# A four-layer Perceiver kernel: earlier weight loads, biases off one-row products, one normalisation for two

## The reference, cut to what matters

```python
x = x + taylor(ln(x))            # L0_attn: causal, features 1, q, q*q; 4 weight matrices, no bias
# L0_ffn, first expert
logits = xt @ router_w + router_b; probs = softmax(logits)
gate, idx = max(probs), argmax(probs)
y = gate * (xt @ expert_w[idx] + expert_b[idx])
# L2_attn, one head over 256 channels
Q, K, V = x @ W1 + b1, x @ W2 + b2, x @ W3 + b3
out = softmax(Q K^T / 16) V @ W4 + b4
# L2_ffn: 8 zone experts, weights w from a router and a temperature
out = sum_e w_e * ((silu(x @ Wg_e) * (x @ Wu_e)) @ Wd_e)
# L3_attn, on ln(x): its own norm again, then two gates and a scan over tokens
normed = (x - mu) * rsqrt(var + EPS) * gamma + beta
z = sigmoid(normed @ Wg.T + bg); c = normed @ Wc.T + bc
h_t = (1 - z_t) * h_{t-1} + z_t * c_t;  out = hs + x
# L3_ffn
out = gelu(x @ w1 + b1) @ w2 + b2
```

## Time and profile before

| | |
|---|---|
| timed runs, median (lowest to highest), us | 1720.31 (1718.38 to 1727.86), 3 runs |
| profiled execution, its own time, us | 1728.6 |
| its span, us, and mean granted clock | 1726.8, 0.931 |
| busy: TensorE, VectorE, ScalarE, GpSimd | 89%, 57%, 42%, 22% |
| granted clock, 40 slices of 43.2 us, in tenths | 9999998799999996579999999889999688999998 |
| DMA busy, the same slices, in tenths | 7668785243453045035554076336660741466401 |

### The profile page before, as it was taken

How to read it: one execution, slowest core, us unless ns; L and a number is a source line. 1 busy time by engine, 2 the same in 40 slices (tenths; PEclk the granted TensorE clock), 3 DMA queues, 4 the chain that set the end, 5 groups by cost and what they waited for, 6 DMA issues and landing times. The chain is left out here.

```text
span 1726.8 us, 30618 instructions
## 1 busy us (share of the span) xinstructions
PE 1538.9 (89%) x11362; PEld 867.1 (50%) x11362; DVE 990.7 (57%) x2293; ACT 716.7 (42%) x961; POOL 381.9 (22%) x543
## 2 busy tenths in 40 slices
PE   6989886899999988979999988589999796999987
PEld 2644644355555555425555555235555464455544
DVE  2434433788888743267777424288884134888831
ACT  3233140244444422025565623147676111676741
POOL 7132140366666620010000012111010000110100
PEclk9999998799999996579999999889999688999998
DMA  7668785243453045035554076336660741466401
GB/s 239 207 218 253 224 258 151 55 70 57 63 73 61 1 82 114 1 65 80 78 78 79 2 240 183 96 71 99 96 98 2 134 147 40 67 100 96 72 19 55
DMA packets 130077, 178.00 MB, mean 103 GB/s; under 512 B 13947, under 2 KB 104972, under 8 KB 122767
## 3 DMA queue, kind: packets, MB, share of 16 engines
q1 hardware_dynamic: 126612, 173.55, 46.1%
q10 hardware_dynamic: 3328, 2.63, 0.6%
HBM read 132.31 MB, written 43.78 MB: 102 GB/s over the span
## 5 line engine op out<-in xcount | busy, mean ns | idle before, releaser
L708 ACT ACTIVATE prob_a<-ps 128x1024 f32<-128x1024 f32 x512 | 505.5, 1023 | 303.2 <-PE ps L593 216.3
L576 PE MATMUL ps<-kop,qop 116*128 116x512 bf16 x1024 | 341.5, 403 | 59.6 <-PEq L431 43.3
L721 DVE CUSTOM_DVE_ANT_0 dump_a<-ps,neg_q 128x512 bf16<-128x512 f32 (+1 forms) x485 | 328.6, 717 | 99.3 <-PE ps L576 97.8
L590 PE MATMUL ps<-qop,kop 116*128 116x256 bf16 x2048 | 349.1, 274 | 5.5 <-ACT prob_a L708 4.9
L725 DVE TENSOR_REDUCE best_a<-ps 128x1 f32<-128x512 f32 (+1 forms) x488 | 312.4, 707 | 58.4 <-PE ps L576 58.3
L590 PEld LDWEIGHTS ps<-qop,kop 116*128 116x128 bf16 x2048 | 194.9, 100 | 137.1 <-ACT prob_a L708 18.3
L576 PEld LDWEIGHTS ps<-kop,qop 116*128 116x128 bf16 x1024 | 86.7, 99 | 220.1 <-issue 99.9
L593 PE MATMUL ps<-neg_k,identb 128*128 128x512 bf16 x512 | 195.7, 382 | 0.0
L615 PE MATMUL ps<-prob_a,vop_a 128*32 128x256 f32 x3072 | 185.0, 382 | 0.0
L820 POOL TENSOR_TENSOR used_a<-prob_a,gT 128x1024 f32<-128x1024 f32 x64 | 151.6, 2369 | 88.1 <-DVE used_a L738 68.0
L311 PE MATMUL ps<-ctxT,wk 128*128 128x512 f32 x256 | 123.2, 628 | 36.8 <-DVE rest L362 23.7
(11 more groups left out here) (296 smaller groups left out, 1422.9 us busy)
## 6 DMA issues: line engine op xcount, KB each, us to landing
kop<-kparts SPq DMA_DIRECT2D x448, 128.0 KB, 5.2
kparts<-kp SPq DMA_DIRECT2D x64, 384.0 KB, 3.7
vals<-vst SPq DMA_DIRECT2D x16, 1024.0 KB, 6.8
vraw<-vals SPq DMA_DIRECT2D x64, 256.0 KB, 6.4
e_w<-in_e_w SPq DMA_DIRECT2D x6, 2048.0 KB, 16.4
z_w<-in_z_w SPq DMA_DIRECT2D x24, 256.0 KB, 5.9
ctxT<-in_ctxT SPq DMA_DIRECT2D x8, 512.0 KB, 9.2
raw<-in_mask SPq DMA_DIRECT2D x8, 512.0 KB, 5.8
```

The costliest lines, as they stand in the source:

```text
L576: return pe.matmul(out, qop[0:R_ALL, h, t * P:(t + 1) * P], kop[0:R_ALL, h % UNROLL, j * CHUNK:(j + 1) * CHUNK], start=True, stop=True)
L590: ins = pe.matmul(st_bank(n)[:, j * NT:(j + 1) * NT], kop[0:R_ALL, h % UNROLL, k * P:(k + 1) * P], qop[0:R_ALL, h, :], start=(j % 2 == 0), ...
L708: act.activation(prob[:, n % NP, :], st_bank(n), ACT.Exp).then_inc(S("exp_done"), 1)
L721: dve.tensor_tensor_reduce(out=dump[:, k % 2, 0:width], in0=bank, in1=c.neg_q[:, t, j * CHUNK:j * CHUNK + width], scale=1.0, scalar=-3.0e3 ...
```

## The change

**Weights.** Five classes (`TaylorWeights`, `FirstExpertWeights`, `PlainWeights`, `ZoneWeights`, `LastWeights` for the last two stages) hold SBUF tiles and semaphores that were inside the stages. They are made before the attention ahead of the stages, and their loads are issued on SP's queue in that attention, behind the operands of the last head. Their semaphores are cleared after the last stage that uses them.

**Biases.** first_expert: the router's bias is added by VectorE as it reads the logits; the experts' biases come from one product of the turned share (8 rows) with the 8 bias rows, after expert 5, added to `x` by VectorE ahead of expert 6. plain_attention: q's bias goes into ScalarE's read (scaled by GpSimd first), k's and v's into VectorE's read, the output's is added to `x` by GpSimd. recurrence: gate biases go into ScalarE's Sigmoid and VectorE's product. feed_forward: the output's bias is added to `x` by GpSimd. q, k and the gates are read in halves of 128 channels, each with its own count.

**Norm.** recurrence takes statistics once. From the variance v of `x` it forms v + EPS and v(1 + EPS) + EPS^2; GpSimd raises both to -1/2 in one instruction; one scale gives the single norm, the other the double. gamma and beta move to ScalarE's copy of the turned tile, one read for each 128 channels.

**Fillers and tables.** 12 filler products are issued during plain_attention's softmax and 12 during recurrence's scan; recurrence's opening fill is 16 products instead of 32. A one-element Exp, Sigmoid or Gelu opens ScalarE's list in plain_attention, recurrence and feed_forward.

The diff, cut to its core:

```diff
+SOFTMAX_FILL, SCAN_FILL = 12, 12
@@ attend, SP
                 ops.load(sp, l, h + UNROLL)
+            if load_next is not None:
+                load_next(sp)
             sp.wait_ge(S("weights"), 32 if l + 1 < LAYERS else 16)
@@ one of the five classes; the others are like it
+class FirstExpertWeights:
+    def load(self, sp):
+        a = self.c.a
+        sp.dma_start(self.router[:, :, :], tiles(a["f_router"])).then_inc(self.S("router"), 16)
+        sp.dma_start(self.router_b[:, :], a["f_router_b"].to_broadcast((P, E))).then_inc(self.S("router_b"), 16)
+        sp.dma_start(self.bias[:, :], a["f_bias"]).then_inc(self.S("bias"), 16)
+        for e in range(E):
+            sp.dma_start(self.w[:, e, :, :], tiles(a["f_w"][e, :, :])).then_inc(self.S(f"expert{e}"), 16)
@@ taylor, TensorE
-            pe.wait_ge(S("weights"), 64)
+            for name in ("q", "k", "v", "o"):
+                pe.wait_ge(weights.S(name), 16)
@@ first_expert, TensorE
             for e in range(E):
-                pe.wait_ge(S(f"expert{e}"), 16)
+                pe.wait_ge(weights.S(f"expert{e}"), 16)
                 if e >= 4:
                     pe.wait_ge(S("added"), QT * (e - 3))
-                by_tokens_pe(c, pe, halves(c, 2 + e % 4), c.xT, w[:, e, :, :], bias[0:1, e, :]).then_inc(S("e_psum"), 1)
+                by_tokens_pe(c, pe, halves(c, 2 + e % 4), c.xT, w[:, e, :, :], None).then_inc(S("e_psum"), 1)
+                if e == TURN_SHARE:     # 3
+                    pe.wait_ge(S("share_found"), QT)
+                    for t in range(QT):
+                        ins = pe.transpose(c.ps[0:E, 6, t * P:(t + 1) * P], share[:, t, :], c.ident[:, :])
+                    ins.then_inc(S("share_turned"), 1)
+                if e == ADD_BIAS:       # 5
+                    pe.wait_ge(S("shareT_ready"), 1)
+                    pe.wait_ge(weights.S("bias"), 16)
+                    for t in range(QT):
+                        ins = pe.matmul(halves(c, 7)[t], shareT[:, t * P:(t + 1) * P], weights.bias[:, :],
+                                        start=True, stop=True)
+                    ins.then_inc(S("bias_psum"), 1)
@@ plain_attention, TensorE
             for k, name in ((0, "q_psum"), (1, "k_psum")):
                 for m in range(CT):
-                    ins = by_channels_pe(c, pe, c.ps[:, 1 + k, m * NT:(m + 1) * NT],
-                                         lambda ct: w[:, k, ct, m * P:(m + 1) * P], c.xT, b[0:1, k, m * P:(m + 1) * P])
-                ins.then_inc(S(name), 1)
+                    by_channels_pe(c, pe, c.ps[:, 1 + 2 * k + m, 0:NT],
+                                   lambda ct: w[:, k, ct, m * P:(m + 1) * P], c.xT).then_inc(S(name), 1)
@@ plain_attention, TensorE, behind the scores
+            keep_warm(c, pe, SOFTMAX_FILL)
             pe.wait_ge(S("p_scaled"), QT)
@@ recurrence, GpSimd, TensorE, VectorE
-            norm_pool(c, pool, S)
-            norm_pool(c, pool, S, 1)
+            pool.wait_ge(S("norm_var"), 2)
+            pool.tensor_tensor(rstd[:, :, :], var[:, :, :], c.minus_half[:, :].unsqueeze(1).to_broadcast((P, 2, QT)), ALU.pow)\
+                .then_inc(S("norm_rstd"), 1)
...
-            keep_warm(c, pe, 2 * NORM_FILL)
-            pe.wait_ge(S("scaled"), 2 * QT)
+            keep_warm(c, pe, NORM_FILL)
+            pe.wait_ge(S("norm_done"), QT)
...
+            keep_warm(c, pe, SCAN_FILL)
             pe.wait_ge(S("scanned"), CT)
...
+            for t in range(QT):
+                dve.tensor_scalar(c.att[:, t, :], c.x[:, t, :], c.moments[:, t, 0:1], rstd[:, 1, t:t + 1],
+                                  ALU.subtract, ALU.mult).then_inc(S("norm_done"), 1)
@@ feed_forward, TensorE
-            by_tokens_pe(c, pe, halves(c, 7), hT, w2, b2[:, :], HT).then_inc(S("out_psum"), 1)
+            by_tokens_pe(c, pe, halves(c, 7), hT, w2, None, HT).then_inc(S("out_psum"), 1)
@@ program
+                    cross(c, 0, True, True, load_next)      # TaylorWeights, FirstExpertWeights
+            cross(c, 2, False, False, load_next)            # PlainWeights, ZoneWeights
+            cross(c, 3, False, False, weights.load)         # LastWeights
```

More of the change, by code:

```diff
@@ L1048, in _, with __init__, load, first_expert @@
             add_stream_dve(c, dve, S, 1)
-def first_expert(c):
+class FirstExpertWeights:
+    def __init__(self, c, ctx):
+        self.c = c
+        self.S = Sems(c.nc, ctx, "first_w")
+        sb = lambda name, shape: ctx.enter_context(c.nc.sbuf_tensor(f"f_{name}", shape, F32))
+        self.router = sb("router", [P, CT, E])
+        self.router_b = sb("router_b", [P, E])
+        self.bias = sb("bias", [E, D])
+        self.w = sb("w", [P, E, CT, D])
+    def load(self, sp):
+        a = self.c.a
[4 more added lines that the diff above has]
+            sp.dma_start(self.w[:, e, :, :], tiles(a["f_w"][e, :, :])).then_inc(self.S(f"expert{e}"), 16)
+def first_expert(c, weights):
     nc = c.nc
+    TURN_SHARE, ADD_BIAS = 3, 5
     with ExitStack() as ctx:
@@ L1056, in first_expert @@
         sb = lambda name, shape, dt: ctx.enter_context(nc.sbuf_tensor(f"f_{name}", shape, dt))
[L1057 to L1060, removed]
+        router, w = weights.router, weights.w
         logits = sb("logits", [P, QT, E], F32)
@@ L1069, in first_expert @@
         share = sb("share", [P, QT, E], F32)
+        shareT = sb("shareT", [E, NT], F32)
         block = ctx.enter_context(nc.Block())
[L1072 to L1078, removed]
         @block.gpsimd
@@ L1816, in zone_experts @@
     FLOOR = 1e-8
[L1817 to L1818 removed]
+    HT = weights.HIDDEN // P
     with ExitStack() as ctx:
@@ L1960, in _ @@
         def _(act):
-            turn_act(c, act, S)
-            act.wait_ge(S("z_psum"), 1)
-            act.activation(z[:, :, :], c.ps[:, 1, :].rearrange("p (m n) -> p m n", n=NT), ACT.Sigmoid)\
-               .then_inc(S("z_ready"), 1)
+            act.activation(warm[:, :], c.ones[:, 0:1], ACT.Sigmoid).then_inc(S("table"), 1)
+            act.wait_ge(S("turned"), 1)
+            act.wait_ge(weights.S("scales"), 16)
+            for ct in range(CT):
+                act.activation(c.xT[:, ct, :], c.ps[:, 0, ct * NT:(ct + 1) * NT], ACT.Identity,
+                               scale=weights.r_gb[:, 0, ct:ct + 1], bias=weights.r_gb[:, 1, ct:ct + 1])\
+                   .then_inc(S("xT_ready"), 1)
@@ L1978, in _ @@
-            dve.wait_ge(S("gates"), 2)
-            for m in range(CT):
+            for m in range(CT):
+                dve.wait_ge(S("z_ready"), m + 1)
+                dve.tensor_scalar(keep[:, m, :], z[:, m, :], -1.0, 1.0, ALU.mult, ALU.add).then_inc(S("gates"), 1)
+            for m in range(CT):
+                dve.wait_ge(S("c_psum"), m + 1)
+                dve.scalar_tensor_tensor(out=zc[:, m, :], in0=c.ps[:, 4 + m, 0:NT],
+                                         scalar=weights.r_bias[:, 1, m:m + 1], in1=z[:, m, :], op0=ALU.add, op1=ALU.mult)\
+                   .then_inc(S("gates"), 1)
+                dve.wait_ge(S("gates"), CT + m + 1)
```

330 lines of the change are left out of this document (207 added, 123 removed).

## The result

| | before | after |
|---|---|---|
| timed runs, median (lowest to highest), us | 1723.89 (1718.38 to 1727.86), 4 runs | 1646.37 (1644.13 to 1649.59), 4 runs |
| ratio, 95% interval | | 0.9554 (0.9517 to 0.9591) |
| profiled execution, its own time; span; granted clock | 1728.6; 1726.8; 0.931 | 1644.13; 1642.4; 0.963 |

What follows compares the result with a forecast made beforehand. It held that the short stages are serial, so ending a wait there moves the kernel's end one for one, several at a low clock. Stage savings summed to 77.7 us off the 1720.3 median, giving 1642.6, range 1634 to 1662.

Steps and rivals of the forecast that it cites:

- Taylor: Taylor stage: weights loaded in attention 0 shrink the 3.28 us wait for t_wo to 0.69; -2.6, bounds -2 to -4.
- first_expert: Stage first_expert: without one-row products and at the high clock, 55.7 us become 22.5; -33.2.
- queries of attention 1: Fill ahead of attention 1 at the high clock, norm decides after 33 names are cleared; -1.2, bounds 0 to -2.2.
- zone_experts: Stage zone_experts: norm no longer late behind the temperature's load, -2.65; clearing 40 names instead of 36 costs +0.3.
- plain_attention: Stage plain_attention: products start 3.05 us earlier and run at the high clock; -24.6.
- recurrence: Stage recurrence: one norm, shorter opening fill, gates at the high clock, filler 0.9 late; 23.1 us shortened by 10.35.
- Moved loads: Loads issued in the attentions behind the last head's operands cost a head nothing: 0, bound +5 in all.
- clock low in a large stage: One-row products go, clock stays low: in one large stage about 1658 us, chance 0.12; in all 1682, chance 0.05.
- hidden costs of 1 to 2 us a stage: Serial stages keep a wait for shareT, overrunning fillers or longer clearings: 1650 us; chance 0.17 together with loads staying on path.
- loads that disturb the attentions: Loads at full DMA rate delay the attentions' operands or engines, making the kernel slower: 1730 us; chance 0.01.
- loads that stay on the path: Taylor, plain and zone keep their load waits: +8, 1651 us; chance 0.17 together with hidden stage costs.
- rival 1: Something other than one-row products holds the clock low: 39 us in all stages, chance 0.05; one large stage, 0.12.

Runs made afterwards that it cites:

- e_rows1: The changed kernel with 16 one-row products added in first_expert, one ahead of each half expert; 1665.21 us, ratio to before 0.9694.
- e_nofill: The changed kernel without the 12 filler products beside plain_attention's softmax and the 12 behind recurrence's gates; 1648.02 us.
- e_late: The changed kernel with each stage's weights loaded at its own start again, all else as changed; 1672.09 us, ratio to before 0.970.
- e_rows1_plain: The changed kernel with one-row products added in plain_attention (8) and recurrence (4), weights still loaded early; 1660.81 us.
- e_twonorms: The changed kernel with recurrence's two norms in succession again, under 32 fill products; 1650.82 us.
- e_drop1: The changed kernel with TensorE made to wait for two GpSimd fills ahead of first_expert's router, plus 16 one-row products before the half experts; 1692.15 us.

## Why the prediction was right

- Taylor: -2.6 forecast, -3.9 measured. The wait went as said. The other 1.3 lies in the per-head products and the tail, whose share at the low clock moved; the sum had left that at nothing, inside its bounds of -2 to -4, and it is within Taylor's own spread of 1.6.
- first_expert: -33.2 against -33.6; the share's chain and the copy of the turned share are hidden as argued, and no product waits for them. The text let the one-row products' going lift the clock, and the clock was lifted; but e_rows1 shows that taking them out was not needed for that in most runs. In money: 12.7 us are the products' own passes and changes, at the high clock; the other 20.9 are the clock and the small edits beside it (the router's pairs gone, the share's turn and bias product added). The size of this term came out for a cause that the text had only in part: one-row products do not put the clock down by themselves, and which part of the change kept it up here stays open. To that extent the number is luck.
- queries of attention 1: -1.0 against -1.2; rstd 3.15 after the last add, 3.14 forecast from 0.07 us for each cleared name. zone_experts' -2.7 likewise, and behind it rstd 3.64 after the last add, 0.3 more than before; the +0.3 of the whole row of attention 3 is within its spread.
- plain_attention: -24.4 against -24.6. Its clock is back for another reason than the one in the text: the load's wait is gone (e_nofill and e_late lower the clock there by an idle time alone, e_rows1_plain does not lower it with the products).
- recurrence: -10.5 against -10.35, with the 0.9 of the late filler; e_twonorms gives the norm 3.5 of it. feed_forward: -3.3 against -3.4.
- Moved loads: 0 forecast, 0 measured.
- The rivals: clock low in a large stage, 0; hidden costs of 1 to 2 us a stage, 0; loads that disturb the attentions, 0; loads that stay on the path, 0. The premise of the first was the sound one, though: something other than the one-row products does put the clock down. The change took out the wait and most changes of row count together. The chance of 0.17 for a low clock in a large stage thus rested on a point that the later runs bear out.
- The text says that the clock carries a third of the gain; its own prices for rival 1 add up to 39 of 77.7, a half. The sum does not hang on that sentence.
- The 3.8 us between 1642.6 and 1646.4 are nearly all the base: the same 77.7 off 1723.9 gives 1646.2.

## What to carry to other kernels

Read a low clock in two steps: what the engine did when it fell (here an idle time of 2.7 to 6.1 us in several places, though 3.28 in Taylor before left it up; and in three places products of fewer rows with no wait over 0.7 us: first_expert and recurrence before, and Taylor's 16-row products), and what keeps it from coming back (here products of 1 or 64 rows between full ones). Take a price from a trace at each level of the clock, since the same pair costs 0.82 at 2.4 GHz and 1.4 at 1.2. A load at a stage's start is hidden by whatever is slow in front of its use: when that becomes fast, move the load too, or the gain comes back as a wait and 2.9 us of slow products. And take filler out again where a run shows that the idle time behind it does not cost the clock: 1.54 us in the scan and 2.51 in attention 2's queries did not, 2.69 in the softmax did. The 3.28 of Taylor, which did not either, shows that the length alone does not tell.

## What the runs showed of the hardware

- One sequence of products runs at either level and keeps the one it has: 29.10 of 29.50 us busy at 1.00 in e_rows1, 53.43 of 54.00 at 0.50 in e_drop1.
- 16-row products against 32-row ones with equal columns: 0.50 and 1.00 in the same ten microseconds of Taylor. The 32 rows are one execution; with 16 the clock falls in all 13 other traces. In after it falls just before 643 (0.50 in the microsecond behind this one), with PE busy throughout:

```profile
642.00:643.00 1.00, 1.00 (x23) 0.76 (x19) 1.00 (x3) 0.84 (x2) 0.00 (x0) 0.86 1.11 148
```

- VectorE's scaling is held up by GpSimd. In e_drop1 two of 0.41 each took 7.17 together, as long as the two fills beside them:

```profile
663.95 7.17 DVE L130 TENSOR_SCALAR xn<-x,moments,rstd 128x256 f32<-128x256 f32 x2 [1.25 <-POOL rstd L137]
```
```profile
663.86 7.11 POOL L1125 MEMSET f_slow<- 128x4096 f32 x2
```

The changed kernel has such a place too, in the queries of attention 2:

```profile
1058.95 4.02 DVE L130 TENSOR_SCALAR xn<-x,moments,rstd 128x256 f32<-128x256 f32 x2 [2.31 <-POOL rstd L137]
1059.09 3.74 POOL L460 TENSOR_SCALAR neg_row_q<-raw_q 1x4096 bf16<-1x4096 uint8 x1 [0.17 <-POOL rstd L137]
```

There the turn of xn waits for it: an estimate of 3.3 us (4.02 less the 0.74 of the same two scalings in plain_attention) that are still to be had, and it was not tried. The Trainium skill (Trainium Architecture — The Big Picture, "What this means for kernel authors") says that VectorE and GpSimd share a pair of ports as an exclusive lock and not as a split of bandwidth; by that the scaling would wait for GpSimd's instruction to end. Both places agree: GpSimd's ends at 670.97 and 1062.83, VectorE's 0.15 later, at 671.12 and 1062.97.
